# A scan kernel whose first pass sums each recurrence step on top of B x in PSUM and takes tanh straight from the banks, one unit behind B

## The chip, the cores and the metric

The kernel runs on one core of one Trainium2 chip. The metric is the device time of one execution in microseconds; lower is better. The core has five engines with a queue of its own each: TensorE (PE, matmuls and transposes), VectorE (DVE), ScalarE (ACT), GpSimd (POOL) and SyncE (SP, which issues DMA here). Each works its queue in the order in which it was written, and the engines wait for each other through semaphores only.

## What is computed

An adaptive-LayerNorm block of two halves on x of 8 x 1024 x 256 in float32. The first half, which the change touches, is a linear recurrence with tanh over 1024 positions; the second is a gated recurrence over rows.

```
h  = layernorm(x) * (1 + ca) + sa
xb = einsum('bsd,ed->sbe', h, B)
for t in 1024 positions:          # h_t = tanh(h_(t-1) @ A.T + xb_t);  y_t = h_t @ C.T
x  = x + ga * layernorm(y + h) (gamma, beta)
h  = layernorm(x) * (1 + cb) + sb
x  = x + gb * tanh(h @ wo.T + c_final @ uo.T + bo)    # c from gates f, i, g over the rows
```

## The kernel before

The 1024 positions of each of the 8 batches are cut into K = 16 chunks of L = 64 positions, so that 8 x 16 = 128 columns step at once. The chunks' starting states are not known at first. A **first pass** runs positions 18 to 63 of every chunk from a state of zero (46 steps, RP1 = 23 pairs of steps); the end state of a chunk becomes the start of the next. The **second pass** then runs all 64 positions from those starts, and a test at its end would repeat the whole if the end states did not agree. In the profiled execution there is one round.

The first pass is written in **units**, one after the other. Unit `ref` has work on several pairs at once, each engine's piece being in `unit1` of that engine:

- LayerNorm of pair ref-1: VectorE takes the statistics and writes (x - mean) * (1 + ca) in two halves (`scalar_tensor_tensor`, L1057); GpSimd adds epsilon (L647) and raises to -0.5 (L649, tile rstdA); ScalarE multiplies each half by it (L815); GpSimd adds sa to each half (L656). SP parks the result in DRAM.
- TensorE transposes pair ref-2 (L1410); ScalarE and VectorE split pair ref-3 into a high and a low part (L796, L1071).
- TensorE multiplies pair ref-4 by B in 12 matmuls (`times_b`, L1391) and ScalarE copies the sums to `state` (L809), which the second pass needs too.
- The recurrence works on pair ref-R1LAG, two steps a unit, `recur1(v, 0, ..)` and `recur1(v, 1, ..)`. A step is four matmuls of 128x128 on A (L1357; each is two instructions in the trace), two of which give the sums of the first half of the features (psR) and two those of the second (psF). VectorE adds xb (`adds1`, L1009, tile pre), ScalarE takes tanh (`tanhs`, L775, tile hs), and the next step's matmuls read it.

GpSimd has besides, after the two adds of some units, one small table instruction (`tables`, lines 632 to 642):

```
                if 6 <= ref < 18:
                    tables(ref - 6)
```

Units 0 to 16 and those from 23 on are written out one by one; units 17 to 22 are a loop of three turns with two units in it. The test above is made when the program is built, so the table of unit 17 stands in the loop's body and runs in units 17, 19 and 21.

From unit 29 on (RP1 + R1LAG) the second pass's steps 2p and 2p+1 are in the units (`step`, L1436), while the last pairs of B are still being made. They begin with the starting states that ScalarE writes in `starts` (L780). `late(i)` transposes the i-th of eight weights of the second half on TensorE (L1319), copies it on ScalarE and splits it on VectorE; the table `LATE1` says in which units. From U0 = 7 on, `unit2` goes on with the second pass and the second half of the block; the change leaves its code as it is.

Of the kernel before, what the change touches and what calls it, by code (L numbers as in the profile page):

```python
# [20 lines left out]
def adaln_kernel(nc, x, A, B, C, gamma, beta, wf, uf, bf, wi, ui, bi, wc, uc, bc, wo, uo, bo, in_c, cond, wmod, out):  # L21
    f32 = mybir.dt.float32
    f32r = mybir.dt.float32r
    i32 = mybir.dt.int32
    ALU = mybir.AluOpType
# [17 lines left out]
    R1LAG = 6  # L43
# [21 lines left out]
    U0 = UNITS1 - RP1 - R1LAG  # L65
    LATE1 = {32: (0, 1), 33: (2, 3), 34: (4, 5), 35: (6, 7)}
# [23 lines left out]
    with ctx:  # L90
# [100 lines left out]
        def bank(name):  # L191
            return ctx.enter_context(nc.psum_tensor(name, [P, 512], f32))

        psR, psC, psT, psF, psI, psG, psW, psO = (bank(n) for n in (
            "psR", "psC", "psT", "psF", "psI", "psG", "psW", "psO"))
# [52 lines left out]
        a_pre = sem("a_pre")  # L248
# [71 lines left out]
                    a_hl, a_sc, a_B, a_xb, a_r, a_pre, a_tanh, a_end, a_start]  # L320
# [288 lines left out]
        def _(pool):  # L609
# [34 lines left out]
            def unit1(v, ref):  # L644
# [107 lines left out]
        def _(act):  # L752
# [19 lines left out]
            def tanhs(v, tt):  # L772
                for m in range(H):
                    act.wait_ge(a_pre, v.lin(4, -4 * R1LAG + 2 * tt + m + 1))
                    act.activation(hs[:, m, :, tt, :], by_chunk(pre[:, m * P:(m + 1) * P]), ACT.Tanh).then_inc(a_tanh, 1)  # L775

            def starts():

                for m in range(H):
                    act.activation(hs[:, m, :, 3, 1:K], by_chunk(pre[:, m * P:(m + 1) * P])[:, :, 0:K - 1], ACT.Tanh).then_inc(a_start, 1)  # L780

            def unit1(v, ref):
                rec, ahead = has(ref, R1LAG, RP1), ref >= RP1 + R1LAG
                p = ref - RP1 - R1LAG
# [6 lines left out]
                if has(ref, 3, PAIRS):  # L791
# [12 lines left out]
                if ref == 4:  # L804
                    act.wait_ge(q_mod, 4)
                    act.activation(mods[:, 2:4, :], psR[0:NB, :].rearrange("b (i d) -> b i d", i=2), ACT.Copy).then_inc(q_col, 1)
                if has(ref, 4, PAIRS):
                    act.wait_ge(a_B, v.lin(1, -3))
                    act.activation(row(pair1(v, ref, 4)), (psW, psO)[ref % 2][:, :], ACT.Copy).then_inc(a_xb, 1)  # L809
# [150 lines left out]
        def _(dve):  # L960
# [44 lines left out]
            def adds1(v, tt):  # L1005
                p = v.lin(1, SP0 - R1LAG)
                for m in range(H):
                    dve.wait_ge(a_r, v.lin(4, -4 * R1LAG + 2 * tt + m + 1))
                    dve.tensor_tensor(pre[:, m * P:(m + 1) * P], (psR, psF)[m][:, 0:P], row(p, m * 2 * P + tt * P, P),  # L1009
                                      ALU.add).then_inc(a_pre, 1)  # L1010

            def unit1(v, ref):
                rec, norm, ahead = has(ref, R1LAG, RP1), has(ref, 1, PAIRS), ref >= RP1 + R1LAG
                p = ref - RP1 - R1LAG
# [47 lines left out]
                if rec:  # L1062
                    adds1(v, 1)
# [615 lines left out]
```

## Time and profile before

| what | value |
|---|---|
| time, median of 3 runs (all) | 581.48 us (580.12 to 581.96) |
| profiled execution: its own time | 581.03 us |
| its span on the core | 579.1 us |
| TensorE, VectorE, ScalarE, GpSimd busy | 554.8, 401.0, 348.8, 361.5 us |
| first pass's steps on TensorE | first starts at 22.6 us, last at 113.8 us of the span |

The span is the time between the first and the last instruction of the profiled execution; 1.93 us lie around it. Busy time is the time in which an engine has an instruction in it, waits left out. Matmul ends are modelled, so TensorE counts as busy over short gaps. In the rows further down, a timeline row gives start, length, engine, line and operation, tile written <- tile read, shapes and number of instructions (x2: two in a row, the length is that of both together), and in brackets the idle time ahead of it with what ended it. A row of a stretch gives the stretch, its length, the busy time of PE, PEld, DVE, ACT and POOL (with counts), the granted TensorE clock as a share of full speed, the DMA share and GB/s. A row of a line's group ends with its busy time, the mean ns of one instruction and the idle time ahead.

### The profile page before, as it was taken

To read this page: it belongs to the slowest core of one execution; us is meant where nothing else is said; L and a number is where in the kernel's file an instruction comes from. 1 tells how busy PE (TensorE), PEld (TensorE's weight loads), DVE (VectorE), ACT (ScalarE), POOL (GpSimd) and SP (SyncE) were. 2 spreads that over 40 slices of the span, in tenths; PEclk is the share of its full clock that TensorE was granted. 3 is DMA by queue.
4 is the path that set the end of the run, shared out by engine and by line. 5 is a ranking of instruction groups with operands and counts; after the bars stand their busy time and mean duration, and the time that the engine had idled before them with its cause. 6 is when DMAs were issued, how large, how long until landed. Compare 5 with 4: busy or idle time off the path is not lost.

```text
span 579.1 us, 13689 instructions
## 1 busy us (share of the span) xinstructions
PE 554.8 (96%) x4616; PEld 536.3 (93%) x4616; DVE 401.0 (69%) x1014; ACT 348.8 (60%) x870; POOL 361.5 (62%) x497
## 2 busy tenths in 40 slices
PE   6999999999988999999999999999999999999992
PEld 3799999989988999999999999999999999999992
DVE  5899999996675666656665666667656576565763
ACT  3767677778357555555665655567565556567550
POOL 4788876675366444444676666667676666768353
PEclk9999999999999999999999999999999999999998
DMA  8555445432433222222214322334333333333244
GB/s 280 159 177 189 126 130 145 135 105 85 137 108 121 65 65 67 83 78 81 79 39 145 92 92 92 95 104 137 112 104 93 92 101 110 101 98 87 63 111 145
DMA packets 58514, 64.10 MB, mean 111 GB/s; under 512 B 5408, under 2 KB 49736, under 8 KB 58448
## 3 DMA queue, kind: packets, MB, share of 16 engines
q1 hardware_dynamic: 58448, 63.26, 36.0%
q8 instruction: 36, 0.59, 0.4%
q14 instruction: 30, 0.25, 0.1%
HBM read 46.44 MB, written 16.81 MB: 109 GB/s over the span
## 4 chain that ended last, share of the span: by engine, by line
PE 72%; POOL 10%; DVE 8%; ACT 4%; issue 3%; DMA 1%; POOLq 0%; DVEq 0%; SPq 0%; ACTq 0%
PE psF L1473 14%; PE psI L1473 14%; PE psG L1473 13%; PE psR L1436 7%; PE psW L1527 7%; POOL hin L656 4%; PE psC L1462 4%; PE psO L1462 3%; PE psT L1508 2%; POOL rstdA L649 2%; DVE hin L1057 2%; ACT hin L815 2%; DVE pre L1009 1%; POOL hsl L665 1%; PE psW L1391 1%
## 5 line engine op out<-in xcount | busy, mean ns | idle before, releaser
L665 POOL TENSOR_TENSOR hsl<-hs,hsh 128x512 fp32r<-128x512 f32 x32 | 41.5, 1296 | 78.5 <-DVE state L1201 41.6
L1189 DVE SCALAR_TENSOR_TENSOR lo<-psT,cb1T,hi 128x256 fp32r<-128x256 f32 x60 | 26.3, 479 | 66.3 <-ACT hi L873 66.3
L656 POOL TENSOR_TENSOR hin<-hin,uvec 128x256 f32<-128x256 f32 x64 | 48.9, 785 | 27.5 <-ACT hin L815 27.5
L1436 PE MATMUL psR<-hs,AT 128*128 128x128 f32 x432 | 62.7, 277 | 2.9 <-ACT hs L832 1.7
L1436 PEld LDWEIGHTS psR<-hs,AT 128*128 128x128 f32 x432 | 54.9, 191 | 4.7 <-ACT hs L832 2.9
L928 ACT ACTIVATE psF<-psF,biasT 128x256 f32<-128x256 f32 x64 | 26.0, 445 | 40.3 <-PE psF L1473 40.3
L1097 DVE TENSOR_TENSOR pre<-psR,state 128x256 f32<-128x256 f32 x44 | 18.6, 423 | 44.4 <-PE psR L1436 44.4
L699 POOL TENSOR_TENSOR zn<-zn,tA 128x512 f32<-128x512 f32 x32 | 41.2, 1288 | 12.4 <-ACT zn L846 12.4
L846 ACT ACTIVATE zn<-state,nmA,rstdA 128x256 f32<-128x256 f32 x64 | 35.0, 594 | 20.0 <-POOL nmA L689 20.0
L1057 DVE SCALAR_TENSOR_TENSOR hin<-xin,mvA,uvec 128x256 f32<-128x256 f32 x56 | 43.0, 806 | 1.7
L712 POOL TENSOR_TENSOR wx<-wx,uvec 128x512 f32<-128x512 f32 x24 | 31.1, 1295 | 18.1 <-DVE state L1201 18.1
L694 POOL TENSOR_TENSOR wx<-wx,tG 128x512 f32<-128x512 f32 x24 | 36.0, 1501 | 9.7 <-ACT wx L894 9.5
L672 POOL TENSOR_TENSOR xin<-xin,tA 128x512 f32<-128x512 f32 x32 | 41.5, 1298 | 0.0
L1357 PE MATMUL psR<-hs,AT 128*128 128x128 f32 x184 | 39.0, 294 | 1.6 <-ACT hs L775 0.9
L815 ACT ACTIVATE hin<-hin,rstdA 128x256 f32<-128x256 f32 x64 | 28.9, 500 | 16.6 <-POOL rstdA L649 16.6
L846 ACT ACTIVATE xn<-state,nmB,rstdB 128x256 f32<-128x256 f32 x64 | 34.8, 590 | 6.8 <-POOL nmB L721 6.8
L775 ACT ACTIVATE hs<-pre 128x128 f32<-128x128 f32 x92 | 23.3, 300 | 23.7 <-DVE pre L1009 23.7
L835 ACT ACTIVATE hs<-pre 128x256 f32<-128x256 f32 x44 | 18.3, 417 | 31.0 <-DVE pre L1097 30.9
L1473 PE MATMUL psF<-hi,wfT_hi 128*128 128x256 f32 x120 | 33.6, 280 | 3.0 <-DVE gf L1209 3.0
L928 ACT ACTIVATE gg<-psG,biasT 128x256 f32<-128x256 f32 x64 | 27.0, 476 | 15.6 <-PE psG L1473 15.6
L1473 PE MATMUL psI<-hi,wiT_hi 128*128 128x256 f32 x120 | 35.7, 298 | 0.0
L1357 PE MATMUL psF<-hs,AT 128*128 128x128 f32 x184 | 35.6, 275 | 0.0
(356 smaller groups left out, 2370.0 us busy)
## 6 DMA issues: line engine op xcount, KB each, us to landing
h_park<-hin SPq DMA_DIRECT2D x32, 256.0 KB, 2.2
hin<-h_park SPq DMA_DIRECT2D x64, 128.0 KB
xin<-in_L_attn_x_dram SPq DMA_DIRECT2D x64, 128.0 KB
tA<-rows_d SPq DMA_DIRECT2D x32, 256.0 KB, 4.5
out_dram<-state SPq DMA_DIRECT2D x64, 128.0 KB
xin<-in_L_attn_x_dram SPq DMA_DIRECT2D x28, 256.0 KB, 2.9
tW<-rows_d SPq DMA_DIRECT2D x32, 128.0 KB, 4.2
tG<-rows_d SPq DMA_DIRECT2D x24, 128.0 KB, 4.2
```

The costliest lines, as they stand in the source:

```text
L656: pool.tensor_tensor(h, h, sa, ALU.add).then_inc(a_h, 1)
L665: pool.tensor_tensor(pair_of(hsl[:, j], t), pair_of(hs, 2 * p % 4), pair_of(hsh[:, j], t).bitcast(f32), ALU.subtract).then_inc(s_hsl, 1)
L672: pool.tensor_tensor(xg, xg, both(tA[:, m % 2, D:W]), ALU.add).then_inc(s_xg, 1)
L699: pool.tensor_tensor(two(zn[:, :]), two(zn[:, :]), both(tA[:, m % 2, 0:D]), ALU.mult).then_inc(s_zg, 1)
L846: act.activation(dst[:, j * D:(j + 1) * D], tiles_of(m)[:, j, :], ACT.Identity, bias=nm[:, j:j + 1], scale=rstd[:, j:j + 1]).then_inc(done, 1)
L928: act.activation(dst[:, m_ * POS:(m_ + 1) * POS], src[:, m_ * POS:(m_ + 1) * POS], fn, bias=biasT[:, i, m_, n % NB:n % NB + 1]).then_inc(s, 1)
L1057: dve.scalar_tensor_tensor(halfw(dst, tt), halfw(src, tt), mv[:, tt, 0:1], ca1, ALU.subtract, ALU.mult).then_inc(a_tmp, 1)
L1357: ins = pe.matmul((psR, psF)[m][:, 0:P], AT[:, k, m * P:(m + 1) * P], hs[:, k, :, 1 - tt, :], start=(k == 0), stop=(k == H - 1), skip_grou ...
L1436: ins = pe.matmul(ps, AT[:, k, m * P:(m + 1) * P], hs[:, k, :, (t - 1) % 4, :], start=(k == 0 and (separate or m == 0)), stop=(k == H - 1 ...
L1462: last = pe.matmul(ps[:, i * D:(i + 1) * D], h[:, j, k, b + i, :, :].rearrange("p t k -> p (t k)"), w["C"][:, k, :], start=(n == 1 and i = ...
L1473: last = pe.matmul(ps[:, at + m * columns:at + (m + 1) * columns], w[name][:, k, m * P:(m + 1) * P], xx[:, k, :], start=(start and n == 1) ...
L1527: last = pe.matmul(ps[:, j * D:(j + 1) * D], h[:, k, j * P:(j + 1) * P], w["wo"][:, k, :], start=(n < HELD and c == 1 and j == 0), stop=(c ...
```

## The change

Two PSUM tensors of two banks each (psWR: psW and psR; psOF: psO and psF) take the place of the four single banks. `times_b` for pair q now leaves the sums of the first half of the features in one bank and those of the second half in the other of the pair (psW, psR) or (psO, psF), by the parity of q. ScalarE copies them to `state` as before, over both banks. Then `recur1` adds its four matmuls onto them (start=False), once ScalarE's copy is done (a_xb), and `tanhs` reads the banks; VectorE's `adds1` and the tile pre are gone from the first pass. The recurrence lags B by one unit instead of two (R1LAG = 5), so that it runs in units 5 to 27; the second pass's steps stay in units 29 and on by a constant of its own, AHEAD = 6. Two late weights are moved from unit 32 to 28.

The core of the diff (declarations and semaphore lists left out):

```
-    R1LAG = 6
+    R1LAG = 5
+    AHEAD = 6
...
-    LATE1 = {32: (0, 1), 33: (2, 3), 34: (4, 5), 35: (6, 7)}
+    LATE1 = {28: (0, 1), 33: (2, 3), 34: (4, 5), 35: (6, 7)}
...
+        psWR, psOF = (ctx.enter_context(nc.psum_tensor(n, [P, 2 * 512], f32)) for n in ("psWR", "psOF"))
+        psC, psT, psI, psG = (bank(n) for n in ("psC", "psT", "psI", "psG"))
+        psW, psR = psWR[:, 0:512], psWR[:, 512:1024]
+        psO, psF = psOF[:, 0:512], psOF[:, 512:1024]
...
+        def sums1(q):
+
+            return ((psW, psR), (psO, psF))[q % 2]
...
             def tanhs(v, tt):
                 for m in range(H):
-                    act.wait_ge(a_pre, v.lin(4, -4 * R1LAG + 2 * tt + m + 1))
-                    act.activation(hs[:, m, :, tt, :], by_chunk(pre[:, m * P:(m + 1) * P]), ACT.Tanh).then_inc(a_tanh, 1)
+                    act.wait_ge(a_r, v.lin(4, -4 * R1LAG + 2 * tt + m + 1))
+                    act.activation(hs[:, m, :, tt, :], by_chunk(sums1(v.c - R1LAG)[m][:, tt * P:(tt + 1) * P]), ACT.Tanh).then_inc(a_tanh, 1)
...
+                def scaled(tt):
+                    if has(ref, 1, PAIRS):
+                        if tt == 0:
+                            act.wait_ge(a_rstd, v.lin(1))
+                        act.wait_ge(a_tmp, v.lin(2, tt - 1))
+                        h = htok(ref - 1)[:, tt * D:(tt + 1) * D]
+                        act.activation(h, h, ACT.Copy, scale=rstd[:, tt:tt + 1]).then_inc(a_sc, 1)
+
                 if rec:
-                    tanhs(v, 1)
-                if ref == RP1 + R1LAG - 1:
-                    starts()
+                    scaled(0)
                 if ahead:
                     step(2 * p + 1)
                     high(p)
...
-                if has(ref, 1, PAIRS):
-                    act.wait_ge(a_rstd, v.lin(1))
-                    for tt in range(2):
-                        act.wait_ge(a_tmp, v.lin(2, tt - 1))
-                        h = htok(ref - 1)[:, tt * D:(tt + 1) * D]
-                        act.activation(h, h, ACT.Copy, scale=rstd[:, tt:tt + 1]).then_inc(a_sc, 1)
...
+                    act.activation(xb, sums, ACT.Copy).then_inc(a_xb, 1)
+                if rec:
+                    tanhs(v, 1)
+                else:
+                    scaled(0)
+                if ref == RP1 + R1LAG - 1:
+                    starts()
+                scaled(1)
...
-                if rec:
-                    dve.wait_ge(a_xb, v.lin(1, 1 - R1LAG))
-                    adds1(v, 0)
...
-                if rec:
-                    adds1(v, 1)
...
             def recur1(v, tt, first):
...
+                if tt == 0:
+                    pe.wait_ge(a_xb, v.lin(1, 1 - R1LAG))
+                for m in range(H):
+                    for k in range(H):
+                        if m == 0 and not first:
+                            pe.wait_ge(a_tanh, v.lin(4, -4 * R1LAG + 2 * tt - 1 + k))
+                        ins = pe.matmul(sums1(v.c - R1LAG)[m][:, tt * P:(tt + 1) * P], AT[:, k, m * P:(m + 1) * P],
+                                        hs[:, k, :, 1 - tt, :], start=False, stop=(k == H - 1), skip_group_check=True)
+                    ins.then_inc(a_r, 1)
...
+                        if ref == RP1 + R1LAG:
+                            pe.wait_ge(a_start, 2)
...
-                times_b(4, 0, 8)
+                times_b(4, 0, 3 * H * H if rec else 8)
                 if rec:
                     recur1(v, 1, False)
-                if ahead:
-                    step(2 * p + 1)
-                times_b(4, 8, 3 * H * H)
+                else:
+                    if ahead:
+                        step(2 * p + 1)
+                    times_b(4, 8, 3 * H * H)
```

ScalarE's queue in one unit of the first pass before, from the first step's tanh to the scaling of the two halves by rstdA (names in brackets are the semaphores it waits for):

```order
L775 ACTIVATE hs<-pre 128x8x16 [waits a_pre] x2
L796 ACTIVATE hi<-psC 128x512 [waits a_B,a_T]
L775 ACTIVATE hs<-pre 128x8x16 [waits a_pre] x2
L809 ACTIVATE state<-psW 128x512 [waits a_B]
L815 ACTIVATE hin<-hin,rstdA 128x256 [waits a_tmp,a_rstd]
L815 ACTIVATE hin<-hin,rstdA 128x256 [waits a_tmp]
```

and the same stretch of the changed kernel (line 782 is the tanh, 803 the high part, 811 the scaling, 828 the copy of B x):

```order
L782 ACTIVATE hs<-psWR 128x8x16 [waits a_r] x2
L803 ACTIVATE hi<-psT 128x512 [waits a_B,a_T]
L811 ACTIVATE hin<-hin,rstdA 128x256 [waits a_tmp,a_rstd]
L828 ACTIVATE state<-psOF 128x512 [waits a_B]
L782 ACTIVATE hs<-psWR 128x8x16 [waits a_r] x2
L811 ACTIVATE hin<-hin,rstdA 128x256 [waits a_tmp]
```

The first scaling has moved up past the copy of B x and the second step's tanh; the second scaling has stayed behind them.

TensorE's queue from the second step of a unit before, through the last four products with B and the transposes, to the next unit's first step:

```order
L1357 MATMUL psR<-hs,AT 128x128
L1357 MATMUL psF<-hs,AT 128x128
L1357 MATMUL psR<-hs,AT 128x128
L1357 MATMUL psF<-hs,AT 128x128
L1391 MATMUL psW<-hi,clo 128x256
L1391 MATMUL psW<-hi,chi 128x256
L1391 MATMUL psW<-lo,chi 128x256
L1391 MATMUL psW<-hi,clo 128x256
L1410 MATMUL psT<-ident,hin 128x128 x4
L1357 MATMUL psR<-hs,AT 128x128
L1357 MATMUL psF<-hs,AT 128x128
```

and in the changed kernel, from the last products with B on:

```order
L1404 MATMUL psWR<-lo,chi 128x256
L1404 MATMUL psWR<-hi,clo 128x256
L1404 MATMUL psWR<-hi,chi 128x256
L1404 MATMUL psWR<-lo,chi 128x256
L1404 MATMUL psWR<-hi,clo 128x256
L1366 MATMUL psOF<-hs,AT 128x128 x4
L1424 MATMUL psT<-ident,hin 128x128 x4
L1320 MATMUL psG<-ident,state 128x8 x4
L1366 MATMUL psWR<-hs,AT 128x128 x4
```

The four products that stood behind the second step now stand ahead of it, and the transposes alone are left between a unit's second step and the next unit's first.

TensorE's queue of the changed kernel at unit 28, the first without a step: the late weight's transposes (line 1327), B (1404), the pair's transposes (1424), the second late weight and the second pass's first step (1450):

```order
L1366 MATMUL psWR<-hs,AT 128x128 x4
L1424 MATMUL psC<-ident,hin 128x128 x4
L1327 MATMUL psG<-ident,wx 128x128 x4
L1404 MATMUL psWR<-hi,chi 128x256
L1404 MATMUL psWR<-lo,chi 128x256
L1404 MATMUL psWR<-hi,clo 128x256
...
L1404 MATMUL psWR<-hi,clo 128x256
L1424 MATMUL psT<-ident,hin 128x128 x4
L1327 MATMUL psI<-ident,wx 128x128 x4
L1450 MATMUL psWR<-hs,AT 128x128
```

GpSimd's queue in the units of the first pass is the same in both kernels: epsilon, power, two adds, table.

## Rows read from the trace of the kernel before

**Rows 1.** Busy time by stage, stretch 22.60 to 95.88 us (columns named in its head).
```profile
22.60:95.88 73.28, 71.68 (x583) 67.24 (x581) 71.36 (x201) 49.53 (x143) 58.65 (x87) 1.00 0.51 157
```

**Rows 2.** Chain of waits, 22 to 116 us, first and last of the GpSimd stretch.
```profile
27.59 1.42 POOL hin L656 x2
...
75.79 0.71 POOL rstdA L649
```

**Rows 3.** Timeline of ScalarE, units 12 and 13 (start us, us, engine, line).
```profile
52.01 0.91 ACT L815 ACTIVATE hin<-hin,rstdA 128x256 f32<-128x256 f32 x2 [0.33 <-POOL rstdA L649]
...
56.17 0.91 ACT L815 ACTIVATE hin<-hin,rstdA 128x256 f32<-128x256 f32 x2 [0.46 <-POOL rstdA L649]
```

**Rows 4.** Timeline of GpSimd, the same stretch.
```profile
52.60 1.60 POOL L656 TENSOR_TENSOR hin<-hin,uvec 128x256 f32<-128x256 f32 x2 [0.62 <-ACT hin L815]
54.17 1.03 POOL L638 TENSOR_SCALAR state<-state 8x256 f32<-8x256 f32 x1
55.17 0.18 POOL L647 TENSOR_TENSOR veA<-mvA,epst 128x2 f32<-128x2 f32 x1
55.44 0.70 POOL L649 TENSOR_TENSOR rstdA<-veA,mhalf 128x2 f32<-128x2 f32 x1
```

**Rows 5.** Timeline of TensorE, unit 26.
```profile
103.45 0.49 PE L1357 MATMUL psR<-hs,AT 128*128 128x128 f32 x2
...
105.40 0.38 PE L1357 MATMUL psR<-hs,AT 128*128 128x128 f32 x2
105.62 0.39 PE L1357 MATMUL psF<-hs,AT 128*128 128x128 f32 x2
...
106.76 0.60 PE L1410 MATMUL psT<-ident,hin 128*128 128x128 f32 x4
...
107.25 0.38 PE L1357 MATMUL psR<-hs,AT 128*128 128x128 f32 x1
```

**Rows 6.** Timeline of ScalarE, GpSimd and VectorE, unit 26.
```profile
103.08 0.51 ACT L775 ACTIVATE hs<-pre 128x128 f32<-128x128 f32 x2 [1.08 <-DVE pre L1009]
103.50 0.58 ACT L809 ACTIVATE state<-psO 128x512 f32<-128x512 f32 x1
103.98 0.90 ACT L815 ACTIVATE hin<-hin,rstdA 128x256 f32<-128x256 f32 x2
...
104.55 1.43 POOL L656 TENSOR_TENSOR hin<-hin,uvec 128x256 f32<-128x256 f32 x2 [1.14 <-ACT hin L815]
...
105.93 0.37 POOL L647 TENSOR_TENSOR veA<-mvA,epst 128x2 f32<-128x2 f32 x1
...
105.21 1.44 DVE L1057 SCALAR_TENSOR_TENSOR hin<-xin,mvA,uvec 128x256 f32<-128x256 f32 x2
```

**Rows 7.** Groups by line, GpSimd, 22.6 to 115.3 us.
```profile
L642 POOL TENSOR_TENSOR wx<-state 8x256 f32<-8x256 f32 x4 | 3.6, 910 | 0.0
...
L632 POOL TENSOR_SCALAR state<-state 8x256 f32<-8x256 f32 x2 | 2.5, 1249 | 0.0
...
L634 POOL TENSOR_SCALAR state<-state 8x256 f32<-8x256 f32 x2 | 2.1, 1028 | 0.0
...
L638 POOL TENSOR_SCALAR state<-state 8x256 f32<-8x256 f32 x2 | 2.0, 1022 | 0.0
...
L636 POOL TENSOR_TENSOR state<-state 8x256 f32<-8x256 f32 x2 | 1.8, 908 | 0.0
```

**Rows 8.** Timeline, ScalarE and TensorE, both ends of the first pass.
```profile
23.20 0.91 ACT L815 ACTIVATE hin<-hin,rstdA 128x256 f32<-128x256 f32 x2 [0.81 <-POOL rstdA L649]
...
26.13 0.51 ACT L775 ACTIVATE hs<-pre 128x128 f32<-128x128 f32 x2 [1.06 <-DVE pre L1009]
...
30.07 0.51 ACT L775 ACTIVATE hs<-pre 128x128 f32<-128x128 f32 x2 [1.21 <-DVE pre L1009]
...
114.50 0.51 ACT L775 ACTIVATE hs<-pre 128x128 f32<-128x128 f32 x2 [1.08 <-DVE pre L1009]
...
115.26 0.49 PE L1436 MATMUL psR<-hs,AT 128*128 128x128 f32 x2 [0.29 <-ACT hs L780]
```

More of the change, by code:

```diff
@@ L1003, in late @@
                                   whi[LATE[i]][:, :, :].bitcast(f32), ALU.subtract).then_inc(q_llo, 1)
[L1005 to L1010, printed above, removed]
             def unit1(v, ref):
-                rec, norm, ahead = has(ref, R1LAG, RP1), has(ref, 1, PAIRS), ref >= RP1 + R1LAG
-                p = ref - RP1 - R1LAG
+                norm, ahead = has(ref, 1, PAIRS), ref >= RP1 + AHEAD
+                p = ref - RP1 - AHEAD
                 src, dst = tile1(ref - 1), htok(ref - 1)
@@ L1301, in batch_rows @@
                 for k in range(H):
-                    last = pe.matmul((psF, psR)[j - 1][0:NB, :], scT[:, k, :], wm[j][:, k, :], start=(k == 0), stop=(k == H - 1))
+                    last = pe.matmul((psF, psO)[j - 1][0:NB, :], scT[:, k, :], wm[j][:, k, :], start=(k == 0), stop=(k == H - 1))
                 last.then_inc(q_mod, 1)
@@ L1350, in recur1 @@
             def recur1(v, tt, first):
-                for k in range(H):
-                    if not first:
-                        pe.wait_ge(a_tanh, v.lin(4, -4 * R1LAG + 2 * tt - 1 + k))
-                    for m in range(H):
-                        if k == 0 and m == 1 and not first:
-                            pe.wait_ge(a_pre, v.lin(4, -4 * R1LAG + 2 * tt))
-                        ins = pe.matmul((psR, psF)[m][:, 0:P], AT[:, k, m * P:(m + 1) * P], hs[:, k, :, 1 - tt, :],
-                                        start=(k == 0), stop=(k == H - 1), skip_group_check=True)
-                        if k == H - 1:
-                            ins.then_inc(a_r, 1)
+                if tt == 0:
[7 more added lines that the diff above has]
+                    ins.then_inc(a_r, 1)
             def unit1(v, ref):
-                rec, ahead = has(ref, R1LAG, RP1), ref >= RP1 + R1LAG
-                p = ref - RP1 - R1LAG
+                rec, ahead = has(ref, R1LAG, RP1), ref >= RP1 + AHEAD
+                p = ref - RP1 - AHEAD
                 if ahead:
@@ L1382, in times_b @@
                             pe.wait_ge(q_wlo, 1)
-                        elif ref > back + 1:
+                        elif not rec and ref > back + 1:
                             pe.wait_ge(a_xb, v.lin(1, -1 - back))
+                        if ref == RP1 + R1LAG:
+                            pe.wait_ge(a_start, 2)
                         pe.wait_ge(a_hT, v.lin(1, 1 - back))
@@ L1389, in times_b @@
                         w, h = ((whi, hmT_hi), (whi, hmT_lo), (wlo, hmT_hi))[n % 3]
-                        ps = (psW, psO)[(ref - back) % 2]
-                        last = pe.matmul(ps[:, m * 2 * P:(m + 1) * 2 * P], w["B"][:, k, m * P:(m + 1) * P],
+                        if ref - back < RP1:
+                            ps = sums1(ref - back)[m][:, 0:2 * P]
+                        else:
+                            ps = (psW, psO)[(ref - back) % 2][:, m * 2 * P:(m + 1) * 2 * P]
+                        last = pe.matmul(ps, w["B"][:, k, m * P:(m + 1) * P],
                                          h[:, (ref - back) % 2, k * 2 * P:(k + 1) * 2 * P],
@@ L1395, in times_b @@
                         last.then_inc(a_B, 1)
-                times_b(4, 0, 8)
+                times_b(4, 0, 3 * H * H if rec else 8)
                 if rec:
                     recur1(v, 1, False)
-                if ahead:
-                    step(2 * p + 1)
-                times_b(4, 8, 3 * H * H)
+                else:
+                    if ahead:
+                        step(2 * p + 1)
+                    times_b(4, 8, 3 * H * H)
                 if has(ref, 2, PAIRS):
```

27 lines of the change are left out of this document (13 added, 14 removed).

## Prediction

> **What bounds the kernel now.** I read the busy times by stage first. From 22.60 to 95.88 us TensorE looks busy for 71.68 of 73.28 us [rows 1], but matmul ends are modelled, so this hides short gaps. I therefore looked for the period of a unit. Unit 26 of the first pass takes 3.80 us from first step to first step (103.45 to 107.25) with TensorE's work end to end [rows 5]; that is TensorE's own length of a unit. Units 12 and 13 are 4.16 us apart (52.01 to 56.17, the scaling by rstdA in each) [rows 3]. So early in the first pass something else is the bound, and the chain of waits says what: from 27.59 to 75.79 us it goes through GpSimd nearly all the time [rows 2].
>
> The loop closes like this: ScalarE's first scaling at 52.01, GpSimd's first add at 52.60 (0.59 later), its table at 54.17 (two adds, 1.57), epsilon at 55.17 (1.00), the power at 55.44 (0.27), the next unit's first scaling at 56.17 (0.73); together 4.16 [rows 3, 4]. The two adds take 1.38 when the first two instructions of VectorE's L1057 are the ones that give way (104.55 to 105.93), so 0.69 each, and 0.88 for the second in unit 12 (1.57 less 0.69) [rows 4, 6]. Where a unit has no table, the loop is short of 3.80 and TensorE decides. There are 14 tables: four of L642 and two of each other line [rows 7] (the two of L640 are as long as those of L636), in units 6 to 17, 19 and 21.
>
> After the first pass nothing that the change touches decides, but for the handover at its end. A delay there moves everything behind it, because the second pass begins with the chunks' starting states.
>
> **What is removed.** VectorE's 92 adds, two for each step, leave the chain from sums to tanh. In unit 26 that chain was covered by TensorE's other work, and in the units with a table GpSimd decides; so I count the removal at nothing, and if some units did wait for these adds, what they give back ends at TensorE's 3.80 (rival 1). The matmuls are the same in number and shape, and SP issues the same transfers in the same units. The copy over two banks has 512 elements as before, 0.58 [rows 6]. Tanh reads PSUM instead of SBUF, and no row has it with 128 elements from PSUM; the bounds I take are 0.1 less or more for each, and the value nothing, since the copy from PSUM (0.58 for 512) and the scaling from SBUF (0.90 for two of 256) are near each other [rows 6]. Two tanhs lie in the loop below, so the bounds are 14 x 0.2 = 2.8 either way.
>
> **TensorE's own period** stays 3.80. Twelve products with B stand in one piece: a step is four pairs 0.22 apart (105.40, 105.62), 0.88, and the eight products take the rest of 1.95, 0.13 each [rows 5]. The second step begins at 1.95 + 4 x 0.13 = 2.47 in the unit. The sums of its first half are there 0.60 later (0.22 and 0.38), at 3.07; a tanh takes 0.30 (0.51 for two that start 0.21 apart [rows 6]): 3.37, needed at 3.80. Those of the second half come 0.44 later, 3.51, tanh to 3.81, needed by the third matmul instruction at 3.80 + 0.32. This leaves 0.3 for semaphores, so I count no wait; the cover behind a second step has however shrunk from four products and the transposes (1.0) to the transposes (0.49), so ScalarE being late by 0.3 would now show.
>
> **What the move on ScalarE costs.** ScalarE's queue now has first scaling, copy of B x, the second step's tanhs, second scaling. GpSimd's second add waits for the second scaling; the next unit's first scaling waits for GpSimd's power; the power stands behind that add and the table. So both ends of the loop now enclose the copy and the tanhs. One turn by rows:
> - second scaling to add: 0.59 [rows 3, 4]
> - second add to what follows it: 0.69, at most 0.88 [rows 4, 6]
> - table: its length less 0.03 (1.03 long, next starts after 1.00) [rows 4]
> - epsilon to power 0.27, power to first scaling 0.73 [rows 3, 4]
> - first scaling to copy: 0.40 (0.90 for two of 0.50) [rows 6]
> - copy to next instruction: 0.48 (103.50 to 103.98) [rows 6]
> - two tanhs to next: 0.42 (103.08 to 103.50) [rows 6]
>
> Sum: 3.58 plus the table (at most 3.77 plus it). Twelve tables in units 6 to 17 are 2 x (1.25 + 1.03 + 0.91 + 1.02 + 0.91) + 2 x 0.91 = 12.1, less 12 x 0.03, 11.7; the two in units 19 and 21 are 1.8 [rows 7]. A unit with a table thus takes some 4.5 where it took 4.16. The other seven of the 21 units between 6 and 27 have 3.58 to 3.77 against TensorE's 3.80, and I take 3.83, since epsilon is 0.37 instead of 0.18 where it meets VectorE [rows 4, 6]. From the tanh of unit 6's second step to that of unit 27: 14 x 3.58 + 11.7 + 1.8 + 7 x 3.83 = 90.4. Before, the same 21 intervals on the same pairs (units 7 to 28) took 114.50 - 30.07 = 84.4 [rows 8]. **Cost 6.0.** What is late next: VectorE's work ahead of the scaling; it must wait for the transposes of the unit before (the slot in hin), which leaves it some 3 us before the scaling asks, so I see no second wait there.
>
> The rows of VectorE and GpSimd in unit 26 start nearly together (105.21; 104.55) and VectorE's pair is 1.44 long [rows 6], while in unit 12 it is GpSimd's second add that is long, 0.91 of the pair's 1.60 [rows 4]. The Trainium skill ("SBUF — State Buffer", section "SBUF: two separate sides") says that the port pair of VectorE and GpSimd is an exclusive lock which whoever starts first holds for the whole instruction. The traces agree in that one of the two pays. By it, the second add pays 0.19 in each unit where L1057 has started first: 14 x 0.19 = 2.7 more. I take no such cost, since the second scaling now comes later and L1057 should be over; the bound is in the range.
>
> **Start.** The recurrence begins in unit 5. Its first scaling waits for the power and starts at 23.20 as before [rows 8]; then copy 23.60, tanhs 24.08, second scaling 24.50, add 25.09, epsilon 25.78, power 26.05, first scaling of unit 6 at 26.78, copy 27.18, tanh 27.66. The same pair's tanh was in unit 7 at 30.07 [rows 8]. **Gain 2.4.**
>
> **End.** Before, from the last second-step tanh (114.50) to the second pass's first step (115.26) it took 0.76 [rows 8], because B and the transposes of that unit lay beside the recurrence. Now unit 28 has no recurrence, and TensorE may start its B only when the starting states are taken (banks psW and psR): four tanhs, 0.42 + 0.42 + 0.1, then twelve products 1.6, transposes 0.49, a late weight's transposes 0.49 [rows 5] (the same shape), 3.5 in all; the first late weight's transposes lie beside the tanhs. **Cost 2.7.** The two late weights are gone from unit 32: 2 x 0.49, **gain 1.0**, at least nothing if that unit then waits, at most 2 if VectorE's and ScalarE's shares of it decided.
>
> **Sum:** 6.0 - 2.4 + 2.7 - 1.0 = +5.3. The span becomes 584.4, with the 1.93 around it 586.3 us, on the profiled execution's 581.03; the median of the runs, 581.48, is 0.45 higher, inside their spread.
>
> **Rivals.**
> 1. *All stalls go, TensorE decides everywhere.* For it: TensorE's 3.80 holds in unit 26, and the change takes instructions out of the recurrence, whatever waited there. Then 21 x 3.80 = 79.8 instead of 84.4, -4.6; with -2.4 + 2.7 - 1.0 the sum is -5.3, **575.7 us**. It needs a turn of the ScalarE-GpSimd loop below 3.80 with its table, against 3.58 + 0.98 by rows. It decides as soon as ScalarE's part of the loop (0.40 + 0.48 + 0.42) were out of it. Chance 0.14.
> 2. *The loop is only half as costly:* a table unit takes 4.2, because tanh from PSUM is 0.1 shorter or the power starts earlier. 14 x 4.2 + 26.8 = 85.6, +1.2; sum +0.5, **581.5**. From there to 4.3 (+1.9) lies a band of cases. Chance 0.10 for no difference, 0.08 for 1.8 to 3 us slower.
> 3. *More late:* the second add pays 0.19 in 14 units (+2.7), or TensorE waits 0.2 for a tanh in the other seven (+1.4), **589 us**. Chance 0.20 for it to reach past 588.
> 4. The main case, 584 to 588: 0.48.
>
> **Numbers.** A measurement of this kernel can tell about 0.3% (1.7 us) from no change. Slower: main, 3 and the band, 0.76; same 0.10; faster 0.14. The range from 580.5 to 590.5 leaves out rival 1 and the tail of 3, together 0.2. The likeliest case's own range is 584 to 588.
>
> **What the changed profile would show.** Unit period by the first scaling near 4.5 in units 6 to 17 and 3.8 from 22 on; ScalarE's idle time in front of the first scaling and released by rstdA, larger than before; GpSimd's second add released by the second scaling, about 1.3 after the first scaling's add could have started; TensorE idle some 0.7 a unit in front of a unit's first step, released by tanh; the second pass's first step near 121.5 instead of 115.26. VectorE has no waits for psR in the first pass. I am wrong if the loop does not run through ScalarE, that is if the idle time ahead of the first scaling is nearly nothing, or if the time lost is in unit 28 alone.

## The result, and the profile after

The changed kernel takes **585.25 us** (median of 4 runs, 584.39 to 585.82), the kernel before on the same chip 580.86 us (4 runs, 580.12 to 581.96): ratio **1.0073**, 95% interval 1.0056 to 1.009. It is 0.7% slower, clear of the spread of the runs. In the profiled executions the span grew from 579.1 to 583.8 us.

From the page of the changed kernel, its busy times, and two groups (line, engine, operation, tiles, shapes, count, busy, mean ns, idle time ahead and its releaser):
```profile
PE 553.8 (95%) x4616; PEld 536.4 (92%) x4616; DVE 374.7 (64%) x922; ACT 348.6 (60%) x870; POOL 356.8 (61%) x497
...
L663 POOL TENSOR_TENSOR hin<-hin,uvec 128x256 f32<-128x256 f32 x64 | 48.3, 760 | 36.9 <-ACT hin L811 35.7
...
L811 ACT ACTIVATE hin<-hin,rstdA 128x256 f32<-128x256 f32 x64 | 31.6, 508 | 31.6 <-POOL rstdA L656 30.9
```
VectorE is 26 us less busy, and the kernel is slower all the same: GpSimd's adds wait 35.7 us for the scalings, and the scalings 30.9 us for GpSimd's power. Two engines that wait for each other are a loop that runs through both, and neither is full.

The same stretch as [rows 1], in the changed kernel:
```profile
22.60:95.88 73.28, 66.97 (x560) 63.91 (x559) 47.99 (x123) 47.79 (x138) 52.63 (x84) 1.00 0.48 148
```
TensorE is busy for 66.97 us where it was 71.68, at the same clock. Here is one turn of the loop, for comparison with [rows 3, 4]. ScalarE's timeline in units 12 and 13:
```profile
54.20 0.51 ACT L811 ACTIVATE hin<-hin,rstdA 128x256 f32<-128x256 f32 x1 [0.99 <-POOL rstdA L656]
54.62 0.58 ACT L828 ACTIVATE state<-psWR 128x512 f32<-128x512 f32 x1
55.10 0.43 ACT L782 ACTIVATE hs<-psOF 128x128 f32<-128x128 f32 x2
55.41 0.52 ACT L811 ACTIVATE hin<-hin,rstdA 128x256 f32<-128x256 f32 x1
...
58.57 0.51 ACT L811 ACTIVATE hin<-hin,rstdA 128x256 f32<-128x256 f32 x1 [1.13 <-POOL rstdA L656]
58.99 0.58 ACT L828 ACTIVATE state<-psOF 128x512 f32<-128x512 f32 x1
59.46 0.43 ACT L782 ACTIVATE hs<-psWR 128x128 f32<-128x128 f32 x2
59.78 0.52 ACT L811 ACTIVATE hin<-hin,rstdA 128x256 f32<-128x256 f32 x1
```
GpSimd's timeline beside it:
```profile
54.79 0.73 POOL L663 TENSOR_TENSOR hin<-hin,uvec 128x256 f32<-128x256 f32 x1 [0.62 <-ACT hin L811]
56.00 0.78 POOL L663 TENSOR_TENSOR hin<-hin,uvec 128x256 f32<-128x256 f32 x1 [0.49 <-ACT hin L811]
56.75 0.85 POOL L645 TENSOR_SCALAR state<-state 8x256 f32<-8x256 f32 x1
57.57 0.18 POOL L654 TENSOR_TENSOR veA<-mvA,epst 128x2 f32<-128x2 f32 x1
57.84 0.70 POOL L656 TENSOR_TENSOR rstdA<-veA,mhalf 128x2 f32<-128x2 f32 x1
```
And TensorE's, where each first step of a unit now stands waiting for a tanh:
```profile
54.56 0.60 PE L1424 MATMUL psT<-ident,hin 128*128 128x128 f32 x4
55.51 1.13 PE L1366 MATMUL psWR<-hs,AT 128*128 128x128 f32 x8 [0.34 <-ACT hs L782]
...
59.87 0.79 PE L1366 MATMUL psOF<-hs,AT 128*128 128x128 f32 x5 [0.47 <-ACT hs L782]
```
Read the turn from 55.41: second scaling, second add at 56.00, table 56.75, epsilon 57.57, power 57.84, next first scaling 58.57, copy 58.99, tanhs 59.46, second scaling 59.78: 4.37 us, where the same unit took 4.16 before.

The ends of the pass, ScalarE first, then TensorE:
```profile
28.55 0.50 ACT L782 ACTIVATE hs<-psOF 128x128 f32<-128x128 f32 x2
...
116.40 0.50 ACT L782 ACTIVATE hs<-psWR 128x128 f32<-128x128 f32 x2
116.80 0.43 ACT L787 ACTIVATE hs<-psWR 128x120 f32<-128x120 f32 x2
```
```profile
117.33 0.36 PE L1404 MATMUL psWR<-hi,chi 128*128 128x256 f32 x1
...
118.84 0.60 PE L1424 MATMUL psT<-ident,hin 128*128 128x128 f32 x4
119.27 0.60 PE L1327 MATMUL psI<-ident,wx 128*128 128x128 f32 x4
119.71 0.39 PE L1450 MATMUL psWR<-hs,AT 128*128 128x128 f32 x2
```
These answer to [rows 8]. The second step's tanhs of unit 6 are at 28.55 (before, unit 7: 30.07), those of unit 27 at 116.40 (unit 28: 114.50), the second pass's first step at 119.71 (115.26). So the 4.45 us by which the second pass starts late are -1.52 at the start, +3.42 over the 21 intervals (87.85 for 84.43) and +2.55 at the handover (3.31 for 0.76). The rest of the program adds 0.2.

### The profile page after: what moved, and what is told of

Read it like the earlier page. It is cut to its first block, busy times and chain, and to the rows that moved or that the text cites. A ratio compares the mean times of both kernels' runs of the same rounds, so it can differ in the third digit from the quotient of the medians.

```text
span 583.8 us, 13540 instructions
## 1 busy us (share of the span) xinstructions
PE 553.8 (95%) x4616; PEld 536.4 (92%) x4616; DVE 374.7 (64%) x922; ACT 348.6 (60%) x870; POOL 356.8 (61%) x497
## 4 chain that ended last, share of the span: by engine, by line
PE 68%; POOL 11%; ACT 7%; DVE 5%; issue 4%; DMA 2%; POOLq 0%; SPq 0%; DVEq 0%; ACTq 0%
PE psOF L1487 13%; PE psI L1487 13%; PE psG L1487 13%; PE psWR L1450 7%; PE psWR L1541 7%; POOL hin L663 4%; PE psC L1476 4%; ACT hin L811 3%; PE psOF L1476 3%; POOL rstdA L656 3%; PE psT L1522 2%; DMA h_park<-hin 1%; ACT state L828 1%; DVE hin L1067 1%; POOL hsl L672 1%
## 5 line engine op out<-in xcount | busy, mean ns | idle before, releaser
L663 POOL TENSOR_TENSOR hin<-hin,uvec 128x256 f32<-128x256 f32 x64 | 48.3, 760 | 36.9 <-ACT hin L811 35.7
L1450 PE MATMUL psWR<-hs,AT 128*128 128x128 f32 x432 | 62.8, 277 | 3.2 <-ACT hs L852 2.4
L1450 PEld LDWEIGHTS psWR<-hs,AT 128*128 128x128 f32 x432 | 54.9, 191 | 5.0 <-ACT hs L852 3.6
L811 ACT ACTIVATE hin<-hin,rstdA 128x256 f32<-128x256 f32 x64 | 31.6, 508 | 31.6 <-POOL rstdA L656 30.9
L948 ACT ACTIVATE psOF<-psOF,biasT 128x256 f32<-128x256 f32 x64 | 25.9, 444 | 40.6 <-PE psOF L1487 40.6
L1105 DVE TENSOR_TENSOR pre<-psWR,state 128x256 f32<-128x256 f32 x44 | 18.6, 423 | 44.3 <-PE psWR L1450 44.3
L1067 DVE SCALAR_TENSOR_TENSOR hin<-xin,mvA,uvec 128x256 f32<-128x256 f32 x56 | 33.7, 642 | 7.4 <-DMA h_park<-hin 3.8
L1487 PE MATMUL psOF<-hi,wfT_hi 128*128 128x256 f32 x120 | 33.7, 281 | 3.0 <-DVE gf L1217 3.0
L893 ACT ACTIVATE hi<-psT,cb1T 128x256 fp32r<-128x256 f32 x60 | 25.0, 467 | 16.5 <-PE psT L1522 16.3
L948 ACT ACTIVATE psI<-psI,biasT 128x256 f32<-128x256 f32 x64 | 26.0, 446 | 14.1 <-PE psI L1487 14.1
L1541 PE MATMUL psWR<-woT_hi,hi 128*128 128x256 f32 x112 | 34.0, 303 | 0.0
```

Source lines behind the costliest of these rows:

```text
L663: pool.tensor_tensor(h, h, sa, ALU.add).then_inc(a_h, 1)
L948: act.activation(dst[:, m_ * POS:(m_ + 1) * POS], src[:, m_ * POS:(m_ + 1) * POS], fn, bias=biasT[:, i, m_, n % NB:n % NB + 1]).then_inc(s, 1)
L1067: dve.scalar_tensor_tensor(halfw(dst, tt), halfw(src, tt), mv[:, tt, 0:1], ca1, ALU.subtract, ALU.mult).then_inc(a_tmp, 1)
L1450: ins = pe.matmul(ps, AT[:, k, m * P:(m + 1) * P], hs[:, k, :, (t - 1) % 4, :], start=(k == 0 and (separate or m == 0)), stop=(k == H - 1 ...
L1487: last = pe.matmul(ps[:, at + m * columns:at + (m + 1) * columns], w[name][:, k, m * P:(m + 1) * P], xx[:, k, :], start=(start and n == 1) ...
L1541: last = pe.matmul(ps[:, j * D:(j + 1) * D], h[:, k, j * P:(j + 1) * P], w["wo"][:, k, :], start=(n < HELD and c == 1 and j == 0), stop=(c ...
```

## The experiments

All were timed in five rounds against the kernel before, which had medians of 580.4 to 581.2 us beside them. The interval of each ratio is 95%. "Period" is the distance between the second steps' tanhs of two units.

**1. Both scalings ahead of the copy.** The changed kernel with the two scalings together again; nothing else moves.
```diff
                 if rec:
                     scaled(0)
+                    scaled(1)
...
-                scaled(1)
+                if not rec:
+                    scaled(1)
```


> The changed kernel with both scalings by rstdA next to each other again, ahead of the copy of B x and the second step's tanhs. Theory A (the loss is the loop ScalarE-GpSimd that encloses the copy and the tanhs between the two scalings): a turn is scaling to add 0.59, two adds 1.38, table 0.98, epsilon to power 0.27, power to scaling 0.73, so 3.95 with a table where the changed kernel has 4.2 to 4.8; 14 units by 0.3 to 0.4 give 4.2 to 5.6 us back: 580 to 581.5 us. Theory B (the cover behind a unit's second step shrank to the transposes, and TensorE waits for tanh whatever the order of the scalings): 585 us, no change from the changed kernel, or slower since tanh comes 0.4 later.

Measured: **577.76 us**, 0.9943 (0.9923 to 0.9962), 7.5 less than the changed kernel. Its ScalarE and GpSimd in the same unit:
```profile
50.14 0.91 ACT L811 ACTIVATE hin<-hin,rstdA 128x256 f32<-128x256 f32 x2 [0.38 <-POOL rstdA L656]
50.95 0.57 ACT L829 ACTIVATE state<-psWR 128x512 f32<-128x512 f32 x1
51.43 0.43 ACT L782 ACTIVATE hs<-psOF 128x128 f32<-128x128 f32 x2
...
54.10 0.91 ACT L811 ACTIVATE hin<-hin,rstdA 128x256 f32<-128x256 f32 x2 [0.33 <-POOL rstdA L656]
```
```profile
50.72 1.41 POOL L663 TENSOR_TENSOR hin<-hin,uvec 128x256 f32<-128x256 f32 x2 [0.62 <-ACT hin L811]
52.10 1.03 POOL L645 TENSOR_SCALAR state<-state 8x256 f32<-8x256 f32 x1
53.10 0.19 POOL L654 TENSOR_TENSOR veA<-mvA,epst 128x2 f32<-128x2 f32 x1
53.37 0.70 POOL L656 TENSOR_TENSOR rstdA<-veA,mhalf 128x2 f32<-128x2 f32 x1
```
The copy and the tanhs are out of the loop: 3.96 a turn instead of 4.37. The loop is the cause. The 21 intervals take 81.47 us, 6.4 less than the changed kernel's 87.85. That is more than I gave this theory, because the units without a table ran mostly at 3.65 us or less and not at the 3.80 that I had called TensorE's own length. The median fell by 7.5 and not by 6.4. In the profiled executions unit 6's tanh stood 1.3 us earlier, at 27.25, and nearly all of that is the start-up, which differs between executions (last section).

**2. The tables on VectorE.** The changed kernel with `tables` in VectorE's queue, so that the loop keeps its straddled scalings and loses its tables.
```diff
 pool:
-                if 6 <= ref < 18:
-                    tables(ref - 6)
 dve:
+                if 6 <= ref < 18:
+                    tables(ref - 6)
```


> The changed kernel with the 14 small table instructions on VectorE instead of GpSimd, nothing else changed; ScalarE keeps the split scalings. Theory A: the loop loses its table and is 3.4 to 3.6 long, TensorE's 3.80 decides in all units; 21 intervals from unit 6 to 27 take 80 instead of 87.9 us: 577 to 578.5 us, clearly faster than both kernels. Theory B (thin cover): 585 us as before. Theory C (the wait for the parked rows' DMA, seen in the chain at unit 23, is what limits): no more than 2 us faster, 583 us.

Measured: **576.48 us**, 0.9929 (0.9907 to 0.9951), the 21 intervals 80.3 instead of 87.85 (3.82 on average). The straddled scalings still cost something without the tables: number 5 below, with the scalings together and the tables on VectorE too, takes 77.14 us for the same 21 intervals and 573.50 us in all, 3 us less. A turn of this kernel's loop, from the second scaling at 51.27 to the next at 55.03, is 3.76 long where I expected 3.4 to 3.6, and so above the 3.65 of number 5. Epsilon is 0.38 us here, not 0.18, and the power follows it 0.46 later instead of 0.27:
```profile
52.55 0.38 POOL L631 TENSOR_TENSOR veA<-mvA,epst 128x2 f32<-128x2 f32 x1
53.01 0.70 POOL L633 TENSOR_TENSOR rstdA<-veA,mhalf 128x2 f32<-128x2 f32 x1
```
With a table in the loop the same straddle costs 6.4 us of intervals (experiment 1), without one 3.2.

**3. Only the straddled scalings, in the kernel before.**
```diff
                 if rec:
+                    scaled(0)
                     tanhs(v, 1)
...
-                    act.wait_ge(a_rstd, v.lin(1))
-                    for tt in range(2):
-                        ...
+                if not rec:
+                    scaled(0)
+                scaled(1)
```


> The kernel before with one part of the change alone: the first scaling ahead of the second step's tanhs and the copy of B x, the second behind them. VectorE's adds, the banks and the lag stay. Theory A: a table unit takes 0.40 + 0.42 + 0.48 + 0.59 + 0.69 + 0.98 + 0.27 + 0.73 = 4.56 instead of 4.0 to 4.16: 12 to 14 units by 0.4 give 5 us slower, 585 to 587 us. Theory B: no change, 581 us, since the cover on TensorE is as before.

Measured: **586.73 us**, 1.01 (1.0079 to 1.0121), 5.9 above the kernel before; units with a table 4.5 to 4.65. Its ScalarE:
```profile
57.58 0.51 ACT L804 ACTIVATE hin<-hin,rstdA 128x256 f32<-128x256 f32 x1 [1.38 <-POOL rstdA L649]
57.99 0.49 ACT L775 ACTIVATE hs<-pre 128x128 f32<-128x128 f32 x2
58.39 0.57 ACT L819 ACTIVATE state<-psO 128x512 f32<-128x512 f32 x1
58.86 0.50 ACT L804 ACTIVATE hin<-hin,rstdA 128x256 f32<-128x256 f32 x1
```
The order on ScalarE alone, without any of the PSUM scheme, costs more than the whole change. The rest of the change is then a gain, as experiment 1 showed (577.8 against 580.9 us).

**4. The late weights back in unit 32.** The changed kernel with one entry of `LATE1` put back.
```diff
-LATE1 = {28: (0, 1), 33
+LATE1 = {32: (0, 1), 33
```


> The changed kernel with the two late weights back in unit 32. The prediction's term says 1.0 us slower than the changed kernel (586.2 us). What the trace of the changed kernel suggests is that from the second pass's first step to unit 36 the same time passes in both kernels (30.6 us), so that the term is nothing: within 0.4 us of 585.25, perhaps 0.4 slower from unit 28 being shorter without them by 0.49 and unit 32 longer.

Measured: **583.99 us**, 1.0051 (1.0031 to 1.0071), which overlaps the changed kernel's interval. The handover took 2.87 instead of 3.31 us, and from the second pass's first step to its eighth unit (150.31 in the changed kernel) 30.57 us against 30.60. Moving them out of unit 32 gained nothing there, and cost 0.4 at the handover. That the median is 1.3 us lower goes with the start-up again: in the profiled executions unit 6's tanh stood at 27.29 instead of 28.55, though the two kernels are the same up to unit 28.

**5 and 6. Both mends in the changed kernel, and the tables' move alone in the kernel before.** Experiment 5 is the edits of 1 and 2 together, 6 the edit of 2 on the kernel before, as its control.

> The changed kernel with both edits that gave time back: scalings next to each other ahead of the copy, and the 14 small table instructions on VectorE. Theory A: ScalarE and GpSimd's loop is 0.59 + 1.38 + 0.27 + 0.73 = 2.97 and never decides; all 21 intervals take TensorE's own length, 3.65 as in the units without a table of the kernel with the scalings together, so 76.7 instead of 81.5 us: 577.76 - 4 = 573 to 574 us. If TensorE instead waits for tanh (thin cover) the units stay near the 3.82 of the kernel with the tables on VectorE: 576 us.

> The kernel before with the 14 table instructions on VectorE, nothing else. Control: how much of what the last kernels gained has nothing to do with the change. If the loop through GpSimd was the bound of its units 9 to 20, they fall from 4.0 to 4.3 to TensorE's 3.80: 21 intervals from 84.4 to some 80 us, 576.5 us. If VectorE, which has the recurrence's adds too, is too full for them (44.27 of 45.5 us busy from 22.5 to 68 us), 579 to 581 us.

Measured: **573.50 us**, 0.9877 (0.9854 to 0.99), and **575.69 us**, 0.991 (0.9889 to 0.9931). Experiment 5 beats both kernels, by 7.6 us (its own comparison) and about 12. Of its 21 units 18 are 3.64 to 3.66 long; those of 6 are 3.80 to 3.83, but for one of 3.88. The four cells:

| | tables on GpSimd | tables on VectorE |
|---|---|---|
| before | 580.9 | 575.7 |
| changed | 585.25 | 576.5 |
| changed, scalings together | 577.8 | 573.5 |

Once the scalings are together, the change is a gain in both columns, 3.1 and 2.2 us.

**7. The late weights back, without the loop.** Experiment 5 with the edit of 4.

> As the kernel with both edits, and the two late weights back in unit 32. In the traces of the changed kernel with and without this, the way from the last tanh to the second pass's first step took 3.31 and 2.87 us, and from there to unit 36 the same 30.6 us: 0.4 us faster than the kernel with both edits. The prediction's term would have it 1.0 us slower.

Measured: **573.66 us**, 0.9871 (0.9847 to 0.9895): no difference to 5 that can be told. The handover takes 3.04 instead of 3.47, and the stretch behind it 30.39 instead of 30.11; what one gives the other takes.

**8. Twelve tables instead of fourteen.** The changed kernel with the tables one unit earlier, so that none stands in the loop's body.
```diff
-                if 6 <= ref < 18:
-                    tables(ref - 6)
+                if 5 <= ref < 17:
+                    tables(ref - 5)
```


> The changed kernel with the tables in units 5 to 16 instead of 6 to 17, so that none stands in the loop's body (units 17 to 22), and 12 run instead of 14: two are gone (19 and 21) and unit 17's is in unit 5. Theory A (a table costs its length in the ScalarE-GpSimd loop, wherever it stands): two turns of 4.63 become 3.65 to 3.8, 1.7 to 2 us faster than the changed kernel, 583.3 us. Thin cover or parked rows: no difference, 585 us.

Measured: **582.79 us** (12 runs), 1.0025 (1.0012 to 1.0038). The units of the loop were 3.63 and 4.63 in turn and are now 3.76 to 3.89. The five intervals behind unit 18's tanh take 18.87 us instead of 20.04, so the two tables that are gone were worth 1.2 us, not their whole length of 1.8: the units without one are now 0.1 to 0.2 us longer. Moving the others by a unit gained nothing: from unit 5's tanh to unit 27's, table of unit 5 included, it is 90.32 us instead of 91.52, the same 1.2. The medians differ by 2.5; in the profiled executions 1.2 us are the start-up (unit 5's tanh at 23.72 instead of 24.88).

**9 and 10. Where does the 0.15 us of a unit come from? More cover behind the second step.** By then two lengths of a unit with the same matmuls were known, 3.65 and 3.80. Theory D: in the kernel before, four products and the transposes behind a unit's second step are too little cover for its tanh. Both kernels are number 6 with the twelve products cut otherwise, seven and five, and six and six.
```diff
-                times_b(4, 0, 8)
+                times_b(4, 0, 7)
...
-                times_b(4, 8, 3 * H * H)
+                times_b(4, 7, 3 * H * H)
```


> The kernel before with the tables on VectorE, and the twelve products with B cut 7 and 5 around the second step instead of 8 and 4. Its units take 3.81 us, those of the kernel with both edits 3.65. Theory D: the 0.15 between them is a wait for tanh at the start of a unit's first step (0.16 and 0.21 us to the first two matmul instructions where 0.11 is the pitch), not work; one product (0.12) more behind the second step hides it: units of 3.65 to 3.70, 572.5 to 573.5 us. Theory E: the 0.15 is what a change of operand kind costs there, whatever waits: 3.81 again, 575.7 us.

> The same with a cut of 6 and 6. Theory D: the wait at the first step stays away, but the second step's tanh is then asked for 0.24 earlier than before and was done 0.2 to 0.25 ahead of it in unit 26: 3.65 to 3.75, 572.5 to 575 us. Theory E: 3.81, 575.7 us.

Measured: **576.47 us**, 0.9924 (0.991 to 0.9937), units 3.80 to 3.91, most of them up to 3.83, and **578.29 us**, 0.995 (0.9938 to 0.9962), units 3.78 to 4.06. One more product of cover changed nothing and two made it worse. Theory D falls; cover isn't what is short.

**11 and 12. Less work on VectorE.** Theory F: VectorE is simply too full. Number 11 is 6, number 12 is 5, with the statistics taken over a quarter of the columns.
```diff
-dve.bn_stats(st[:, tt, :], halfw(tile1(ref), tt)).then_inc(a_stats, 1)
+dve.bn_stats(st[:, tt, :], halfw(tile1(ref), tt)[:, 0:64]).then_inc(a_stats, 1)
```


> The kernel before with the tables on VectorE, and the first pass's LayerNorm statistics taken over 64 of the 256 columns of each half; three quarters of that work is left out, two VectorE instructions a unit become about 0.16 to 0.2 us shorter each, everything else stands. The cuts 7 and 5 and 6 and 6 did not move the unit from 3.80, so the 0.15 is no wait that cover on TensorE could hide. Theory F: VectorE itself is the bound there (3.74 of 3.81 us busy, back to back), and TensorE's own length is 3.65: units of 3.65 to 3.70, 572.5 to 573.5 us. Theory G: the recurrence's own way from sums through VectorE's add and tanh, twice a unit, is 3.80 long, whatever else VectorE does: 575.7 us.

> The control: the same statistics over 64 columns in the changed kernel with both edits, where VectorE is busy for 2.5 of 3.65 us. Theory F: TensorE decides already, no change, 573.5 us with units of 3.65. If shorter statistics help by some other way (LayerNorm's chain), it is faster here too.

Measured: **576.92 us**, 0.9932 (0.9912 to 0.9952), units still 3.81, and **573.45 us**, 0.9871 (0.9847 to 0.9896), units 3.65. Theory F falls as well. What is left can be read in number 11, where VectorE now has slack. VectorE:
```profile
98.38 0.34 DVE L1024 BATCH_NORM_STATS2 stA<-xin 128x6 f32<-128x64 f32 x2
99.11 0.29 DVE L1007 TENSOR_TENSOR pre<-psR,state 128x128 f32<-128x128 f32 x1 [0.39 <-PE psR L1357]
99.32 0.28 DVE L1007 TENSOR_TENSOR pre<-psF,state 128x128 f32<-128x128 f32 x1
99.52 0.24 DVE L1042 BATCH_NORM_AGGREGATE mvA<-stA 128x2 f32<-128x6 f32 x2
99.83 1.44 DVE L1055 SCALAR_TENSOR_TENSOR hin<-xin,mvA,uvec 128x256 f32<-128x256 f32 x2
101.19 0.28 DVE L1007 TENSOR_TENSOR pre<-psR,state 128x128 f32<-128x128 f32 x1
```
Its TensorE, and its ScalarE:
```profile
98.06 0.49 PE L1357 MATMUL psR<-hs,AT 128*128 128x128 f32 x2
...
100.02 0.38 PE L1357 MATMUL psR<-hs,AT 128*128 128x128 f32 x2
...
101.38 0.60 PE L1410 MATMUL psT<-ident,hin 128*128 128x128 f32 x4
101.87 0.49 PE L1357 MATMUL psR<-hs,AT 128*128 128x128 f32 x2
```
```profile
101.51 0.51 ACT L750 ACTIVATE hs<-pre 128x128 f32<-128x128 f32 x2 [1.07 <-DVE pre L1007]
```
The idle 0.39 us stands ahead of the first step's add (99.11), while the second step's add (101.19) starts without a gap behind the scaling of the LayerNorm (L1055 here, L1057 before). The chain closes: first step 98.06, its add 1.05 later, the second add of the two, aggregates and L1055 0.72 later, the pair 1.36, tanh 0.32, next first step 0.36: 3.81, the unit's length. No view names a wait of VectorE there, since it is busy with L1055 when the sums come. It explains why neither cover nor shorter statistics moved anything: neither is in the chain. This reading agrees with the unit lengths of 6, 9, 11 and of the kernel before, but no run tested it by itself (L1057 written behind the second step's adds would), so it stays argued.

## Why the prediction was right, and where it wasn't

**The side and the main case held.** The time lies in the main case's 584 to 588, and the mechanism is the one that the prediction gave: both ends of the loop now enclose the copy and the tanhs, experiments 1 and 3 taking it out and putting it in.

**"Cost 6.0" for the 21 intervals measured 3.4.** The turn without its table was 3.55 (0.59 + 0.75 + 0.27 + 0.73 + 0.42 + 0.47 + 0.32), predicted 3.58: the second add was 0.06 longer than taken, the two tanhs to their next 0.32 and not 0.42. The tables were what was mis-sized: I took their lengths from [rows 7], 0.91 to 1.25, but nine of the twelve in units 6 to 17 were 0.72 to 0.86 long in the changed kernel, as in the row at 56.75. In the kernel before they began beside the end of VectorE's L1057 and had its adds beside them; when those nine begin, L1067 is over. The twelve units took 52.6 instead of 54.7, the nine others 35.2 instead of 35.8.

**"Gain 2.4" at the start measured 1.5.** The first scaling of unit 5 started at 23.98 and not at 23.20 as I had assumed, in an execution whose start-up was longer (last section). In experiment 2 it started at 23.15 and unit 6's tanh stood at 27.72, 2.35 before the 30.07. From the scaling to that tanh the changed kernel took 4.57, predicted 4.46, so the path was right. Number 6 has the kernel before's first pass with the same long start-up as the changed kernel, and its tanh stood at 30.31, 1.8 later than 28.55. The term lies between 1.8 and 2.4; a single execution does not fix it better.

**"Cost 2.7" at the end measured 2.55.** Its parts are right to within 0.2: two pairs of tanhs 0.40 and then 0.53 to the first product, products and the two sets of transposes 2.38.

**"Gain 1.0" by the late weights measured nothing.** The step that fails is the removal counted at TensorE's time: [rows 5] gives the length of the transposes, and nothing I read said that TensorE decides in unit 32. Experiment 4 shows the same 30.6 us with and without them. The lower bound that I gave, nothing, is what held.

**The sum** 3.4 - 1.5 + 2.55 + 0.2 = 4.7 stands against 5.3: a cost 2.6 smaller than I had it and two gains 0.9 and 1.0 smaller mostly cancelled. That the time came out so close is luck in this, and the mechanism held without it.

**The signs.** Three were met: scalings and adds that wait for each other, no wait of VectorE for psR, and the second add 1.2 us behind the first (1.3 predicted). The units with a table were 4.2 to 4.8 long, 4.4 on average, not 4.5; TensorE's idle time ahead of a first step was 0.34 to 0.47 in the rows above and not 0.7; and the second pass's first step came at 119.71, not near 121.5, as the sizes of the terms have it.

**"Unit 26 takes 3.80 us ... that is TensorE's own length" was wrong,** and with it "I count the removal at nothing". In experiment 5 the four transposes ahead of a first step take 0.44 us and its eight matmuls 0.81 (53.12, 53.56, 54.37); in [rows 5] and in number 11 it is 0.49 and, in number 11, 0.92 (98.06 to 98.98). The 0.16 us is a wait for tanh which the modelled ends of the matmuls cover up. The 0.32 that the prediction took from a step's start to its third instruction holds part of the same wait. Experiment 5's TensorE:
```profile
53.12 0.60 PE L1426 MATMUL psC<-ident,hin 128*128 128x128 f32 x4
53.56 1.06 PE L1368 MATMUL psOF<-hs,AT 128*128 128x128 f32 x8
54.37 0.36 PE L1406 MATMUL psWR<-hi,chi 128*128 128x256 f32 x1
```
What the change removes is thus worth about 0.15 us in each of the units that TensorE decides, some 3 us in all: the 21 intervals take 77.14 us in number 5 and 80.05 in number 6. By the chain read in number 11 it is VectorE's adds that are worth it. The change moves the banks and the lag along with them, and no run took these apart. In the changed kernel nearly all units were ScalarE's and GpSimd's, so it was not collected.

**The rivals.** Rival 1 (all stalls go) named the point from which it decides, ScalarE's part being out of the loop. That point is right: experiment 1 reached 577.8, and without the tables 573.5. Its price of 575.7 stood on 3.80. Rival 2's price for a unit with a table, 4.2, was met in four of the twelve. Rival 3's first cost did not come: the second adds are mostly 0.72 to 0.81 long, not 0.88. It is not that they never meet VectorE's L1067, as the prediction assumed. In most units its last 0.19 us lie beside the add, which is then 0.78 long against 0.72 with nothing beside it (at 34.24). At 73.22 the add gave way, 0.87 long with the end of L1067 (0.88 for the pair, from 72.61) beside it; near 77 us it was L1067:
```profile
77.29 1.36 DVE L1067 SCALAR_TENSOR_TENSOR hin<-xin,mvA,uvec 128x256 f32<-128x256 f32 x2 [0.47 <-DMA h_park<-hin]
...
77.63 0.74 POOL L663 TENSOR_TENSOR hin<-hin,uvec 128x256 f32<-128x256 f32 x1 [0.49 <-ACT hin L811]
```
The rule of the Trainium skill ("SBUF — State Buffer", section "SBUF: two separate sides") is that whoever starts first holds the port pair for the whole instruction. These rows agree with it in that one of the two pays; no run here set the two starts apart on purpose, so they show no more than that.

## What to carry to other kernels

When an instruction is moved within an engine's queue, look for the loop that closes through it: work between two halves of a producer lies in every turn of the loop if the consumer's queue feeds back to the first half, though neither half needs it. Take an engine's own length of a stage from the pitch of its instructions where nothing could hold them, not from a row of busy time, and price instructions by rows in which the neighbours are as they will be. A change can hold a gain and a loss of which the loss is one line's place: undo its parts one by one before it is dropped.

## What the runs showed of the hardware

- The start-up differs between executions. A row of four 8x512 matmuls near 12 us took 3.08 us in the profiled execution of before, 3.58 in that of the changed kernel and in number 6, 3.29 in number 2, and 1.88 in numbers 1, 3, 4 and 5, though their streams are alike there. TensorE's pace changes at about that time, and not at the same time in each: ahead of the row four transposes took 1.37 us in the changed kernel, where number 1 had two in 0.44 (10.24); behind it four took 0.63 (16.41). The granted clock is 1.00 on both sides, and what sets the moment is open. It moved unit 6's tanh by up to 1.3 us and shows in the times: four runs of number 6 took 575.4 to 575.9 us and two 577.5 and 577.7, the profiled one of 3.58 among the two. Differences of 1 to 2 us between medians of a few runs therefore say little here, and the intervals of the first pass say more. The changed kernel's rows and number 1's:
```profile
10.69 1.37 PE L1424 MATMUL psT<-ident,hin 128*128 128x128 f32 x4 [0.47 <-POOL hin L663]
12.00 3.58 PE L1310 MATMUL psOF<-state 128*8 128x512 f32 x4
```
```profile
11.47 1.88 PE L1312 MATMUL psOF<-state 128*8 128x512 f32 x4
```
- A tanh of 128x128 from PSUM is 0.28 long, and two with their data ready are over in 0.43 where the two from SBUF took 0.51 [rows 6].
- Most of GpSimd's small tables are 0.72 to 0.86 long where VectorE is idle or nearly so beside them, and 0.91 to 1.03 where it works [rows 4, 7]; the first of all is 1.25 in both kernels. That the neighbour is the cause is argued from where the rows stand, not tried.
- VectorE's L1067 waits in the changed kernel five times, 3.8 us in all, for the transfer that parks a LayerNorm result (h_park). The chain of waits shows it once as 4.26 us at 103.12, and no experiment touched it.
